# Sums of query squares with the squares as moving operand, and new orders on four engines, in a fused attention kernel

## What is computed

```
q = x @ Wq;  k = ctx @ Wk;  v = ctx @ Wv          16 heads of 128
q = q * rsqrt(mean(q^2) + 1e-5) * gq;  k likewise with gk
x = x + tanh(g) * softmax(q k^T / sqrt(128)) v @ Wo
x[batch 0] = x + tanh(g) * mixture of 16 experts (352 inner columns, 4 experts per row)
```

## Time and profile before

| | |
|---|---|
| median of 3 runs | 1547.44 us (1547.04 to 1547.54) |
| the profiled execution, its own time | 1550.0 us |
| its span in the trace | 1548.1 us |
| mean granted TensorE clock | 0.987 |
| busy: PE, VectorE, ScalarE, GpSimd | 96%, 68%, 64%, 54% of the span |
| chain that ended last: PE, VectorE, ScalarE | 85%, 7%, 3% of the span |

### The profile page before, as it was taken

One profiled execution on the slowest core, in us unless ns is written; L12 is line 12 of the kernel. 1 busy time (PEld: TensorE's weight loads), 2 busy tenths in 40 slices (PEclk: granted clock), 3 DMA queues, 4 the chain that ended last, 5 costly groups with the idle time before them and its releaser, 6 DMA issues.

```text
span 1548.1 us, 24699 instructions
## 1 busy us (share of the span) xinstructions
PE 1489.4 (96%) x8506; PEld 1277.6 (83%) x8506; DVE 1053.1 (68%) x2061; ACT 991.3 (64%) x2238; POOL 837.2 (54%) x662
## 2 busy tenths in 40 slices
PE   5988889999999999999999999999999999999997
PEld 3777768888888788888888888888888887888885
DVE  7776565666666767676676776766767676687665
ACT  6764446766676567666666666676766765666654
POOL 3443244555555447566666666665757655564331
PEclk9999979999999999999999999999999999999999
DMA  6310001111111323443334333343433331331002
GB/s 238 123 49 15 1 21 42 44 54 41 48 42 41 109 89 131 132 133 121 119 118 138 127 127 117 126 138 123 131 122 122 124 130 36 94 89 35 8 1 82
DMA packets 53369, 138.60 MB, mean 90 GB/s; under 512 B 5312, under 2 KB 5312, under 8 KB 53248
## 3 DMA queue, kind: packets, MB, share of 16 engines
q1 hardware_dynamic: 49488, 124.71, 24.6%
q0 software_dynamic: 3760, 12.32, 2.8%
HBM read 122.60 MB, written 14.42 MB: 89 GB/s over the span
## 4 chain that ended last, share of the span: by engine, by line
PE 85%; DVE 7%; ACT 3%; issue 2%; POOL 2%; DMA 0%; POOLq 0%; SPq 0%; ACTq 0%; DVEq 0%
PE j_bank L431 11%; PE j_bank L433 11%; PE j_bank L432 11%; PE w_bank L431 10%; PE w_bank L433 9%; PE w_bank L432 9%; PE t_bank L510 7%; PE s_bank L431 4%; PE s_bank L433 4%; PE s_bank L432 4%; PE t_bank L587 2%; PE t_bank L576 2%; PE t_bank L586 1%; DVE stats L984 1%; PE w_bank L618 1%
## 5 line engine op out<-in xcount | busy, mean ns | idle before, releaser
L816 ACT ACTIVATE prob<-s_bank,neg_bias,q_scale 128x512 f32<-128x512 f32 x256 | 198.5, 776 | 348.4 <-DVE neg_bias L1206 347.8
L980 DVE TENSOR_TENSOR probT_lo<-t_bank,probT_hi 128x512 fp32r<-128x512 f32 x264 | 179.5, 690 | 198.0 <-ACT probT_hi L718 198.0
L1245 DVE SCALAR_TENSOR_TENSOR x_sb<-w_bank,inv_sum,x_sb 128x512 f32<-128x512 f32 x256 | 187.6, 743 | 2.2 <-PE w_bank L433 2.2
L1190 DVE TENSOR_REDUCE neg_max<-s_bank 128x1 f32<-128x512 f32 x256 | 169.0, 681 | 5.6 <-PE s_bank L433 5.6
L510 PE MATMUL t_bank<-ident,prob 128*128 128x128 f32 x1024 | 154.6, 274 | 3.9 <-DVE probT_lo L980 2.0
L718 ACT CAST probT_hi<-t_bank 128x512 fp32r<-128x512 f32 x264 | 152.9, 593 | 1.7 <-PE t_bank L510 1.7
L431 PE MATMUL j_bank<-wkv_lo,cT_hi 128*128 128x256 f32 x512 | 146.0, 285 | 3.7 <-issue 2.4
L1389 POOL TENSOR_TENSOR sqs_lo<-xn,sqs_hi 128x512 fp32r<-128x512 f32 x64 | 83.3, 1302 | 118.7 <-ACT xn L874 118.6
L433 PE MATMUL j_bank<-wkv_hi,cT_lo 128*128 128x256 f32 x512 | 146.0, 285 | 0.0
L432 PE MATMUL j_bank<-wkv_hi,cT_hi 128*128 128x256 f32 x512 | 145.7, 285 | 0.0
L510 PEld LDWEIGHTS t_bank<-ident,prob 128*128 128x128 f32 x1024 | 122.5, 141 | 24.2 <-issue 3.3
(11 more groups left out here) (241 smaller groups left out, 4543.7 us busy)
## 6 DMA issues: line engine op xcount, KB each, us to landing
stage<-w SPq DMA_DIRECT2D x96, 256.0 KB, 3.0
xnT_raw<-w_gu SPq DMA_DIRECT2D x31, 704.0 KB, 4.2
cT_raw<-w_gu SPq DMA_DIRECT2D x31, 704.0 KB, 4.8
xnT_raw<-w_dn SPq DMA_DIRECT2D x16, 768.0 KB, 4.4
cT_raw<-w_dn SPq DMA_DIRECT2D x15, 768.0 KB, 4.8
planes<-bits SPq DMA_DIRECT2D x16, 512.0 KB, 4.0
y<-stage SPq DMA_DIRECT2D x31, 256.0 KB, 4.4
x_sb<-x SPq DMA_DIRECT2D x5, 1024.0 KB, 8.0
```

Of the source, the lines that this page charges most:

```text
L816: nc.scalar.activation(prob[:, i, :], s_bank[i % 2][:], ACT.Exp, bias=neg_bias[:, u % 2, i:i + 1], scale=q_scale[:, u % 2, i:i + 1], accum ...
L980: return nc.vector.tensor_tensor(dst, src, hi, ALU.subtract)
L1190: nc.vector.tensor_reduce(neg_max[:, u % 2, i:i + 1], s_bank[i % 2][:], AX_X, ALU.max, negate=True).then_inc(own_max, 1)
L1245: nc.vector.scalar_tensor_tensor(out=here, in0=w_bank[0 if packed else i % 2][:], scalar=inv_sum[:, w % 2, i:i + 1], in1=here, op0=ALU.mul ...
```

## The change

On PE the squares were the stationary operand (128 x 128) and a 2-column block of ones the moving one; eight products gave the sums, one query row per partition. Now the stationary operand is one column of ones, read 128 times, and the squares are the moving operand, 512 columns wide, high and low part: two products. Every partition of `t_bank[0]` then holds the sums of all 512 query rows. VectorE multiplies this with the identity, repeated four times, and reduces each group of 128, which leaves each partition its own four sums. The product goes into `sq`, so ScalarE's second square waits for `q_ss_out`.

The orders change too. PE: `gate_up(0)` stands ahead of `probs(0)`. ScalarE, packed: `values_hi` stands ahead of `softmax(0)`. VectorE, packed: `rows_to_lo` and `copy_y` come before `squares_out`, and `inverses` and `values_lo` between it and `shift(0)`. VectorE, unpacked: `squares_out` stands ahead of the two maxima, and the last add of an item, `add(3)`, is done in the next step behind `values_lo` (not for steps 17, 19, 20 to 51 and 65).

```diff
+def deferred(t):
+
+    return not (T0 <= t <= T0 + NB) and t not in (LAST[0] + 2, T0 - 1, NI + 1)
...
@@ PE, query_squares @@
-                    for i in range(NT):
-                        here = slice(i * P, (i + 1) * P)
-                        pe.matmul(t_bank[0][:, 2 * i:2 * i + 2], sqs[0][:, here], ones[:], start=True, stop=False)
-                        last = pe.matmul(t_bank[0][:, 2 * i:2 * i + 2], sqs[1][:, here], ones[:], start=False,
-                                         stop=True)
-                    last.then_inc(q_ss_mm, 1)
+                    every_row = ones[:, 0:1].to_broadcast([P, P])
+                    pe.matmul(t_bank[0][:], every_row, sqs[0][:], start=True, stop=False)
+                    pe.matmul(t_bank[0][:], every_row, sqs[1][:], start=False, stop=True).then_inc(q_ss_mm, 1)
@@ PE, step @@
                 key_value(0)
+                gate_up(0)
                 probs(0)
                 scores(2)
-                gate_up(0)
                 key_value(1)
@@ ScalarE, query_squares @@
-                    need(act, sq_lo, 1, u, 1)
+                    need(act, q_ss_out, 1, u, 1)
@@ ScalarE, step @@
                 rows_to_hi()
+                if packed:
+                    values_hi()
                 softmax(0)
...
-                if packed:
-                    values_hi()
                 key_value_rows(0)
@@ VectorE, squares_out @@
-                    nc.vector.tensor_scalar(q_ss[:, u % 2, :], t_bank[0][:, 0:2 * NT:2], HD * EPS, None,
-                                            ALU.add).then_inc(q_ss_out, 1)
+                    own = sq.rearrange("p (i q) -> p i q", i=NT)
+                    nc.vector.scalar_tensor_tensor(
+                        out=own, in0=t_bank[0][:].rearrange("p (i q) -> p i q", i=NT), scalar=HD * EPS,
+                        in1=ident[:].unsqueeze(1).to_broadcast([P, NT, P]), op0=ALU.add, op1=ALU.mult).then_inc(
+                            q_ss_own, 1)
+                    need(dve, q_ss_own, 1, u, 1)
+                    nc.vector.tensor_reduce(q_ss[:, u % 2, :], own, AX_X, ALU.add).then_inc(q_ss_out, 1)
@@ VectorE, step @@
-                maximum(0)
-                maximum(1)
                 if packed:
+                    maximum(0)
+                    maximum(1)
                     gate_up_lo()
-                    inverses()
+                    rows_to_lo()
                     copy_y()
                     squares_out()
-                    rows_to_lo()
+                    inverses()
+                    values_lo()
                     shift(0)
                     shift(1)
                 else:
                     squares_out()
+                    maximum(0)
+                    maximum(1)
                     shift(0)
                     shift(1)
                     inverses()
...
-                values_lo()
+                if not packed:
+                    values_lo()
+                if deferred(t - 1):
+                    add_before(3)
                 probs_lo(0)
...
-                    add(3)
+                    if not deferred(t):
+                        add(3)
```

More of the change, by code:

```diff
@@ L251, in flamingo_kernel @@
         kT_mm, kT_hi, kT_lo = sem("kT_mm"), sem("kT_hi"), sem("kT_lo")
-        q_mm, q_hi, q_lo, q_squared, sq_lo, q_ss_mm, q_ss_out, q_scale_ready = (
-            sem("q_mm"), sem("q_hi"), sem("q_lo"), sem("q_squared"), sem("sq_lo"), sem("q_ss_mm"), sem("q_ss_out"),
-            sem("q_scale_ready"))
+        q_mm, q_hi, q_lo, q_squared, sq_lo, q_ss_mm, q_ss_own, q_ss_out, q_scale_ready = (
+            sem("q_mm"), sem("q_hi"), sem("q_lo"), sem("q_squared"), sem("sq_lo"), sem("q_ss_mm"), sem("q_ss_own"),
+            sem("q_ss_out"), sem("q_scale_ready"))
         s_mm, s_max, p_exp, p_turned, p_hi, p_lo = (
@@ L1236, in values_rows, with add_of @@
                                           kv_raw[:, :, HD:2 * HD]).then_inc(v_hi, 1)
-                def add(i):
-                    if not value:
+                def add_of(w, i):
+                    if w < 0:
                         return
@@ L1247, in add, with add_before @@
                         in1=here, op0=ALU.mult, op1=ALU.add).then_inc(w_added, 1)
+                def add(i):
+                    add_of(w, i)
+                def add_before(i):
+                    add_of(w - 1, i)
                 def query_lo():
```

## The result

| | before | with the change |
|---|---|---|
| median of 4 runs each | 1547.49 us (1547.04 to 1549.62) | 1574.62 us (1573.27 to 1577.59) |
| ratio, 95% interval | | 1.0175 (1.0158 to 1.0193) |
| span of the profiled execution | 1548.1 | 1571.5 |
| busy: PE, VectorE | 96%, 68% | 93%, 72% |

The account below looks back on a forecast made before the run. PE's own work was taken to set the end, with packed steps passing to the chain through VectorE's held cast. Terms +27.9 - 1.0 - 4.4 = +22.5 us made a span of 1570.6, forecast time 1570, range 1547 to 1586.

Parts of the forecast that it names:

- The sum: Whole kernel: packed +27.9, unpacked with new weights -1.0, without -4.4, together +22.5 us, a span of 1570.6.
- PE's narrow products: Query squares on PE: two wide products take 0.46 instead of 0.90 for eight narrow ones, 0.44 us less a step.
- VectorE's diagonal: Identity product and reduction on VectorE: 1.46 us until the sums are there, bounds 0.8 and 2.2.
- Unpacked steps with new weights: t = 2 to 17 and 54, 57, 60, 63: bias slightly earlier, -0.05 us each, -1.0 in all.
- Unpacked steps without new weights: Nine of t = 52 to 64, and t = 1: the full 0.44 us comes through 10 times, -4.4.
- Packed steps: t = 20 to 50: probs(0) later, cast held by GpSimd, add(0) late; +0.9 us each, +27.9 for 31.
- What hangs on probs(0) moves with it: Packed steps: probs(0) goes from S + 9.02 to S + 10.49, probs_hi(0) to 11.12; the exponential is ready 0.8 before.
- PE setting the pace everywhere: Rival, every step: PE still sets the pace, the change gives 64 x 0.44 = 28 us, 1519; chance 0.15.
- The cast that isn't held: Rival, packed steps: GpSimd doesn't hold the cast, -0.3 us each, 1533; chance 0.04 of 0.10 shared with half-held.
- its half-held form: Rival, packed steps: cast held half the time, +0.25 us each, 1550; chance 0.05 of 0.10 shared with free cast.
- The diagonal at its upper bound: Rival: diagonal takes 2.2, unpacked steps with new weights 0.7 us longer; 1585 or more; chance 0.07, shared with delayed expert-weight loads.
- the slow wide products: Rival, query squares on PE: wide products take twice the time, PE gains nothing, 1588; chance 0.03.

Follow-up runs that it names:

- sums_behind: The changed kernel with the sums behind the two maxima in unpacked steps, as before the change: 1594.6 us.
- no_deferral: The changed kernel with add(3) of an unpacked step back at the end of its own step: 1577.4 us.
- early_only: The changed kernel with ScalarE's copies of wo and wq ahead of values_hi and softmax(0), the cast left in place: 1560.6 us.
- gate_up_first: The kernel before with one edit, gate_up(0) ahead of probs(0) in packed steps: 1588.0 us.
- sums_only: The kernel before with the two wide products, the diagonal and ScalarE's wait for q_ss_out, every order as it was: 1614.4 us.
- cast_late: The changed kernel with VectorE's cast of the values (kv_hi) behind shift(3) instead of ahead of add(0) in packed steps: 1529.9 us.
- gate_up_back: The changed kernel with gate_up(0) back behind probs(0) and scores(2): 1574.8 us.
- late_and_early: The changed kernel with the packed steps' cast behind shift(3) and ScalarE's copies of wo and wq ahead of values_hi and softmax(0): 1518.2 us.
- cast_one_port: The changed kernel with the packed steps' cast replaced, at the same place, by a reduction over groups of one element: 1547.5 us.

## Why the prediction was right, point by point

**The sum.** The span grew by 23.4 us where 22.5 were forecast. The packed steps carry it as forecast: from the squares of t = 21 to those of t = 51 the change loses 28.8. But the rest agrees by luck as well. The step from t = 51 to 52 lost 1.7 and the end behind the squares of t = 64 lost 0.8, which the forecast had at nothing; against that the changed kernel was 5.7 ahead at t = 21, of it 2.5 with the clock of t = 2, and won 2.1 from t = 52 to 64. The forecast had 5.4 of gains and no such losses.

**PE's narrow products.** Right: 0.46 for the two wide ones with the load behind them covered, and an unpacked step without new weights lost 0.44. That the weights are one column read 128 times costs nothing. The spacing stayed at 0.23; the 0.13 of the Trainium skill (TensorE: Matmul & The Clock Gate, "Back-to-back issue gap") does not hold for these products.

**VectorE's diagonal.** Right, and a little dear: 0.71 from the start of the product with the identity to that of the reduction and 0.69 for it, 1.40 where 1.46 was taken.

**Unpacked steps with new weights.** The sign was right and the term too small: -0.05 a step was forecast and -0.18 measured for t = 3 to 17, 2.7 us over these 15 steps. One unpacked step, whose S is 277.88:

```profile
279.95 0.69 DVE L1200 SCALAR_TENSOR_TENSOR xn<-t_bank,ident 128x512 f32<-128x512 f32 x1 [0.35 <-PE t_bank L591]
280.67 0.69 DVE L1205 TENSOR_REDUCE q_ss<-xn 128x4 f32<-128x512 f32 x1
281.27 1.28 DVE L1192 TENSOR_REDUCE neg_max<-s_bank 128x1 f32<-128x512 f32 x2
282.48 0.33 DVE L1213 TENSOR_SCALAR neg_bias<-neg_max,q_scale 128x1 f32<-128x1 f32 x2
```

The sums are done at S + 3.48, as worked out (284.19 - 280.71). The step of the working that was off is the last one, the bias: `q_scale` was done at S + 4.57 (4.62 forecast), and the bias followed at 4.60 instead of 4.73, since VectorE came to it straight from the maxima and not out of a wait, as the missing bracket shows; before it was 4.76. `sums_behind` and `no_deferral` show that what holds the step at 17.2 is indeed this chain, and `early_only` that ScalarE's weight copies in it are worth another 0.43.

**Unpacked steps without new weights.** Right in size (17.18 to 16.74 in the stretch above), though for fewer steps: t = 58, 59, 61 and 62 gained 0.42 to 0.47 each, but the six from t = 52 to 57, two of them with a new `wo`, gained 0.1 us together (1418.00 - 1313.12 = 104.88 before, 1442.65 - 1337.84 = 104.81 now, by the starts of the query squares). What holds them wasn't tried. The step from t = 51 to 52 went from 20.31 to 21.96, which the prediction had at no change. It is 20.34 in `gate_up_first` and 21.11 in `sums_only`, so the move alone doesn't cause it and the sums cause a part; `cast_late` (21.42) and `early_only` (21.44) take some of it back, and the rest stays open.

**Packed steps.** +0.97 measured, +0.9 forecast, and the times inside the step agree: `probs(0)` at S + 10.47 (10.49 forecast), the cast 1.52 (1.52), `add(0)` at 16.68 (16.51), `project_out(1)` at 17.47 (17.31), `project_out(3)` at 24.22 (24.06), which is the 0.16 that the forecast put on two steps of three. From `add(0)` to the end of `add(2)` 7.48 were measured and 7.49 taken over from before. The forecast took `add(0)` at S + 15.10 before from a step with a short hold, and the step's length, 24.05, from the mean of all; since it added up the changed step afresh and only subtracted that mean, this did no harm.

**One sentence of it was wrong as a cause.** "What hangs on probs(0) moves with it", and the exponential "is no hindrance": `gate_up_back` shows that without the move `probs_hi(0)` is as late, held by ScalarE's own row of work behind the late `q_scale`, in the two steps of three with a copy of a weight. The prediction checked whether the exponential was ready for PE, and not when ScalarE would have come through the exponentials and the two copies behind it.

**The rivals.** PE setting the pace everywhere (1519) fell for the change as made and came true in `late_and_early` (1518.2), once the cast and the copies were moved. The cast that isn't held (1533) was close to `cast_late` (1529.9), where it is moved, and its half-held form (1550) is about what `cast_one_port` measured, 1547.5, with a cast of 0.67. The diagonal at its upper bound and the slow wide products did not occur.

## What to carry to other kernels

A busy share of 96% says which engine works, not how far behind it the next loop runs: add up that loop before a saving on the busy engine is booked, because here 0.44 us saved on PE turned into 0.97 lost per step. When two edits each delay the same successor, undoing one proves nothing about it; look at what the successor's own engine does ahead of it. Here a VectorE copy of fp32 from SBUF to SBUF that began beside a long GpSimd operation ended only behind that operation, in all 31 cases. Where a trace shows such a pair, try a later place for the copy, or an operation that isn't held.

## What the runs showed of the hardware

The hold isn't new with the change: the cast took up to 1517 ns before as well. In the trace it is no idle time in front of the instruction but a longer instruction, so no list of waits shows it. What was not expected is how completely it can be avoided with the same data: 674 to 689 ns for the reduction in all 32 packed steps, slower than the free cast's 415 and faster than the held one. Moved behind `cT_round`, the cast is never held at all. All 64 of them, in the kernel before:

```profile
L1235 DVE CAST kv_hi<-kv_raw x64: 415/430/1517, 193.8 to 1512.9; 128x512 fp32r<-128x512 f32 x64
```

And in `cast_late`:

```profile
L1242 DVE CAST kv_hi<-kv_raw x64: 415/417/446, 194.1 to 1493.1; 128x512 fp32r<-128x512 f32 x64
```

The granted clock makes its own difference from one execution to another. Of 19 executions of the kernel before on one chip, the four with a mean granted clock of 0.988 or more are the four fastest, 1546.7 to 1547.0 us; the other 15, at 0.984 to 0.987, took 1547.8 to 1550.8.
